# Graph attention on one core: SyncE's row fetches spread over ten turns, VectorE's block loop written out, four widened one-hots in the last block

## The chip, the cores and the metric

The kernel runs as one launch on one core of a Trainium2 chip. The core has five engines that run their own instruction streams and meet only at semaphores: TensorE (PE, with its weight loads shown apart as PEld), VectorE (DVE), ScalarE (ACT), GpSimd (POOL) and SyncE (SP), which computes nothing and issues transfers. The metric is the time of one execution on the device in microseconds (us). Changes of this kernel's time by less than 0.2% are not told from no change.

## The reference, cut to what matters

A graph of 3125 nodes with 128 features and 100000 edges passes through four graph networks. The second (L1) has three attention layers, and the change touches these alone. One layer computes, with edges sorted by destination:

```
xl, xr = h @ Wl + bl, h @ Wr + br                # per node, 4 heads of 32
e      = leaky_relu(xl[dst] + xr[src])           # per edge
logit  = sum over a head's 32 of e * att
alpha  = softmax of logit over the edges of one destination node
out    = segment_sum(alpha * xr[src], dst)
```

Every edge also has the pair of a node with itself, which the kernel adds apart.

## The kernel before, in words

**Tiles.** 125 edges make a tile (one edge per partition), four tiles a quad, so there are 200 quads. The destinations fall into 25 windows of 125 nodes. A step handles one quad for one window; a quad on the border of two windows is handled twice, which gives 224 steps, in 14 blocks of 16 steps. A group is four steps.

**Rows of the sources.** `xr[src]` is gathered row by row (132 numbers: 128 features and 4 more) into `rows`, a ring of 20 quads. GpSimd gathers (`gather_wide`, L615): one indirect DMA fills one tile, and in nine quads out of ten it fetches 128 rows, not 125. The three rows too many, for 36 tiles, are 108 rows of the last tile of the tenth quad, so that quad needs only three gathers. Ten such quads are called a share here (`SHARE`), and SyncE's work on one quad a turn. A layer has 780 gathers.

**SyncE** (`pass_wide`) is the ring's clerk. In each turn q it first frees an old quad: it loads from a table which step uses quad q-18 last, waits until VectorE has weighed it, and raises `kept` (L630). GpSimd waits for `kept` before each quad and may by this be at quad q+2. Then SyncE waits until the rows of quad q have landed and raises `here` (L654), for which VectorE waits. In turn 8 of a share it copies the 108 spare rows into the tenth quad with three DMAs (`hand_over`, L634), and the 17 rows still missing (`ALONE`) it fetches one by one, each with a register loaded from a table (`fetch_alone`, L642): nine in turn 7, behind `here`, and eight in turn 8, behind the hand-over. In turn 9 it waits for all twenty before it raises `here`. After every fourth turn it loads the next list of sources (L625). All this is one stream in order.

**One step on VectorE** has six operations: `z` = destination part (from PSUM `zp`) + rows (L982); `values` = rows times the weights of the step 16 earlier (`weigh`, L995); the leaky relu and the product with `att` (L985); the sum of another earlier step added to `acc` (`add_team`, L1003); the reduction over each head (L988); the logits (L991). Ring slots and windows are run-time numbers, and VectorE loads them into registers for four steps together: 12 numbers ahead of the group's first `z` (`step_places`) and 8 between that and its `weigh` (`step_pairs`).

**One block**: 16 steps, then `softmax(b)`, a chain of small operations that goes back and forth between VectorE, TensorE and ScalarE, up to L1041. There VectorE waits for TensorE (L923, L924), writes `tail` and scales `acc` (L1045 to L1054). In block b the logits of block b and the weighing of block b-1 go side by side. Block 0 only has logits, and behind the last block the 16 steps of weighing stand alone (`close`).

**TensorE** turns one-hots: `spread_rows` (L893) makes `zp` for the next step; `sum_rows` (L903) adds the weighted rows of a step into `sums` with f32 one-hots. **ScalarE** issues the loads of the one-hots from memory (L826, L830) and widens one (bf16 to f32, L835) into one of two buffers `hot32` when the sum two steps earlier is done. A load of a one-hot goes out two steps ahead of its use.

Of the kernel before, what the change touches and what calls it, by code (L numbers as in the profile page):

```python
# [618 lines left out]
def pass_wide(nc, sp, g, table, rows, now, lone, lone_in, staged, rows_in, given, here, kept, step_done, held_up):  # L619

    early = ALONE // 2 + 1
    assert HELD >= GIVING + SHARE - 1 and RING - HELD <= GIVING - 6
# [9 lines left out]
    def hand_over(q):  # L632
        for e in range(EXTRA):
            sp.dma_start(rows[GIVERS * e:GIVERS * (e + 1), q, HALF - 1, :],  # L634
                         rows[P + e:P + e + 1, q - GIVING:q, :, :].rearrange("p a j f -> p (a j) f")).then_inc(given[q // SHARE], 16)

    def fetch_alone(share, q, lo, hi):
# [82 lines left out]
def step_places(nc, eng, g, k, n=AHEAD):  # L720

    _, got = nc.values_load_multi_w_load_instructions(g.place[0:1, bass.ds(3 * k, 3 * n)], engines=(eng.engine,), min_val=0, max_val=QUADS - 1,
                                                      skip_runtime_bounds_check_because="prepare counts them from the step and its window")
    slots = [nc.s_assert_within(v, 0, RING - 1, skip_runtime_bounds_check_because="prepare takes it modulo the ring") for v in got[1::3]]
    wins = [nc.s_assert_within(v, 0, WIN - 1, skip_runtime_bounds_check_because="prepare counts them up from 0, one for each later window") for v in got[2::3]]
    return list(zip(got[0::3], slots, wins))
# [28 lines left out]
def attention(nc, g, table, xl, xr, ft, own_att, own_logit):  # L755
# [4 lines left out]
    with Scope(nc) as sc:  # L760
        rows = sc.sb("rows", [LANES, RING, HALF, ROW])
        now = sc.sb("now", [LANES, STAGES, HALF * HALF], I32)
        lone = sc.sb("lone", [1, QUADS // SHARE * ALONE], I32)
        hot_t = sc.sb("hot_t", [P, AHEAD, HALF * P], BF16)
# [12 lines left out]
        hot32 = sc.sb("hot32", [P, 2, HALF * P])  # L777
        spare = xl[:, :, :].rearrange("p w f -> p (w f)")
# [18 lines left out]
        factor = turn[0:P, 1, 256:256 + D]  # L797
        turned_weights = turn[0:P, 0, 0:HEADS * BT].rearrange("p (h s) -> p s h", h=HEADS)
# [7 lines left out]
        given = [sc.sem(f"given{n}") for n in range(RING // SHARE)]  # L806
        staged = [sc.sem(f"staged{n}") for n in range(STAGES)]
# [7 lines left out]
        @block.sync  # L815
        def _(sp):
            pass_wide(nc, sp, g, table, rows, now, lone, lone_in, staged, rows_in, given, here, kept, weighted, fetching)

        @block.scalar
        def _(act):  # L820
# [11 lines left out]
            def widen(c, m, i, q):  # L832
                act.wait_ge(hot_in[q], landed(m))
                act.wait_ge(closed, after(c, 2))
                act.copy(hot32[:, q % 2, :], hot[:, q, :]).then_inc(made, 1)  # L835
                act.copy(values[:, q % 2, :, D:ACCW], tail[:, bass.ds(HALF * AHEAD * i + HALF * q, HALF), :]).then_inc(tailed, 1)

# [27 lines left out]
            with act.Fori(1, BLOCKS) as b:  # L865
                with act.Fori(0, GROUP) as i:
                    group(b, i)
                weigh(b)
            last = TEAMS - BSTEPS
            with act.Fori(0, GROUP - 1) as i:  # L870
                for q in range(AHEAD):
                    c = last + AHEAD * i + q
                    widen(c, last // AHEAD + i, i, q)
                    load_hot(c + 2, (q + 2) % AHEAD)
            for q in range(AHEAD):
                widen(TEAMS - AHEAD + q, TEAMS // AHEAD - 1, GROUP - 1, q)
                if q < 2:
                    load_hot(TEAMS - AHEAD + q + 2, q + 2)
# [4 lines left out]
        def _(pe):  # L883
# [12 lines left out]
            def sum_rows(c, q):  # L896
                p = q % 2
                pe.wait_ge(made, after(c))
# [3 lines left out]
                for j in range(HALF):  # L902
                    ins = pe.matmul(sums[:, p, 0:ACCW], hot32[:, p, j * P:(j + 1) * P], values[:, p, j, :], start=j == 0, stop=j == HALF - 1)  # L903
# [45 lines left out]
            with pe.Fori(0, GROUP) as i:  # L949
                for q in range(AHEAD):  # L950
                    sum_rows(TEAMS - BSTEPS + AHEAD * i + q, q)

        @block.vector
        def _(dve):
            begin(dve, added, scaled, reduced, summed, weighted, accd)
            link = Link(dve, step)
            link(dve.tensor_copy(factor, own_att))
            for w in range(0, WIN, FIVE):
# [17 lines left out]
            def logits(k, i, q, source):  # L976
                p, s = q % 2, bass.ds(HALF * AHEAD * i + HALF * q, HALF)
                quad, at, _ = source
# [26 lines left out]
            def softmax(b):  # L1005
# [36 lines left out]
                dve.sem_inc(shifted, 1)  # L1042
                first = g.first[:, bass.ds(BT * b, BT)]
# [19 lines left out]
            softmax(0)  # L1063

            def both(b, i):
                first = isinstance(i, int) and i == 0
                for q in range(AHEAD):
                    k = BSTEPS * b + AHEAD * i + q
                    c = k - BSTEPS
                    if q == 0:  # L1070
# [1894 lines left out]
```

## Time and profile before

| what | value |
| --- | --- |
| three runs | 5736.91, 5737.38 (median), 5743.67 us |
| the profiled execution | 5733.8 us, its span 5731.7 us |
| mean granted TensorE clock | 0.799 of full speed |
| the three attention layers, from the first gather to the last sum | 1046.1 to 2177.7, 2231.4 to 3362.6, 3417.5 to 4548.9 us |

The profile shows the profiled execution in microseconds from the start of its span. Each of the layers takes 1131 us, so the part that the change touches is 3394 us of 5732. Busy shares of a whole span average over parts that have nothing to do with each other; an engine's idle time in front of an instruction, and what ended it, say more.

### The profile page before, as it was taken

To read this page: it belongs to the slowest core of one execution; us is meant where nothing else is said; L and a number is where in the kernel's file an instruction comes from. 1 tells how busy PE (TensorE), PEld (TensorE's weight loads), DVE (VectorE), ACT (ScalarE), POOL (GpSimd) and SP (SyncE) were. 2 spreads that over 40 slices of the span, in tenths; PEclk is the share of its full clock that TensorE was granted. 3 is DMA by queue.
4 is the path that set the end of the run, shared out by engine and by line. 5 is a ranking of instruction groups with operands and counts; after the bars stand their busy time and mean duration, and the time that the engine had idled before them with its cause. 6 is when DMAs were issued, how large, how long until landed. Compare 5 with 4: busy or idle time off the path is not lost. (4 is left out here: it accounts for less than half of the span.)

```text
span 5731.7 us, 121544 instructions
## 1 busy us (share of the span) xinstructions
PE 3638.7 (63%) x28023; PEld 3144.2 (55%) x28024; DVE 4068.1 (71%) x8991; ACT 1470.8 (26%) x3625; POOL 2966.9 (52%) x3112
## 2 busy tenths in 40 slices
PE   6887886455555553555565544555555555999985
PEld 5774443355545543545455534555555444999984
DVE  8998523677777777777777777777777657777754
ACT  4775200011111111111111110111111211555553
POOL 0000000566766753767766717767667204777773
PEclk9998997577777776677877766777777777999997
DMA  5883452244434432334444423444434222555552
GB/s 154 220 220 105 129 142 70 67 106 104 104 101 100 105 88 61 99 100 100 104 106 104 103 50 93 104 102 102 102 101 102 56 56 71 144 145 144 144 137 74
DMA packets 528864, 618.70 MB, mean 108 GB/s; under 512 B 123778, under 2 KB 465602, under 8 KB 528740
## 3 DMA queue, kind: packets, MB, share of 16 engines
q0 software_dynamic: 110400, 232.13, 17.7%
q10 hardware_dynamic: 254649, 235.22, 13.8%
q1 hardware_dynamic: 163691, 149.87, 10.0%
q8 instruction: 56, 0.92, 0.1%
q14 instruction: 68, 0.56, 0.0%
HBM read 521.60 MB, written 91.69 MB: 107 GB/s over the span
## 5 line engine op out<-in xcount | busy, mean ns | idle before, releaser
L615 POOL DMA_INDIRECT rows<-row_table,now x2340 | 2269.7, 970 | 1791.3 <-issue 1498.4
L903 PE MATMUL sums<-both,hot 125*125 125x137 f32 x5376 | 1018.9, 345 | 902.1 <-DVE acc L1003 718.6
L903 PEld LDWEIGHTS sums<-both,hot 125*125 125x125 f32 x5376 | 871.5, 235 | 985.3 <-DVE acc L1003 555.4
L600 POOL DMA_INDIRECT rows<-node_table,now x700 | 664.0, 949 | 507.6 <-issue 504.9
L893 PE MATMUL zp<-parts,hot_t 125*125 x8100 | 790.0, 263 | 206.4 <-DVE z L982 110.4
L893 PEld LDWEIGHTS zp<-parts,hot_t 125*125 125x125 bf16 x8100 | 756.0, 173 | 241.2 <-issue 239.6
L835 ACT CAST hot<-hot 125x500 f32<-125x500 bf16 x672 | 408.7, 608 | 1818.0 <-PE sums L903 1630.9
L982 DVE TENSOR_TENSOR z<-zp,rows 125x528 f32<-125x528 f32 x672 | 475.6, 708 | 489.6 <-issue 158.8
L995 DVE TENSOR_TENSOR both<-rows,turn 125x512 f32 (+1 forms) x672 | 457.2, 681 | 89.6 <-issue 46.3
L1278 PE MATMUL mixture<-row_parts,at 125*125 125x384 bf16 x2500 | 446.1, 330 | 45.2 <-DVE at L1335 45.2
L988 DVE TENSOR_REDUCE both<-z 125x16 f32<-125x512 f32 x672 | 457.3, 680 | 4.4
L985 DVE SCALAR_TENSOR_TENSOR z<-z,turn 125x512 f32<-125x512 f32 x672 | 457.7, 681 | 1.7
L1335 DVE TENSOR_TENSOR at<-spread_srcs,nodes 125x1625 bf16<-125x1625 f32 x200 | 356.6, 1784 | 65.0 <-PE mixture L1278 43.9
L1278 PEld LDWEIGHTS mixture<-row_parts,at 125*125 125x125 bf16 x2500 | 330.4, 138 | 104.3 <-issue 25.7
L1614 DVE TENSOR_SCALAR hot<-nodes,both 125x522 bf16<-125x522 f16 x896 | 315.2, 416 | 20.9 <-PE bank L1653 20.7
L1653 PE MATMUL bank<-hot,hot_dst 125*125 125x261 bf16 x1792 | 261.3, 290 | 69.8 <-DVE hot L1614 48.6
L1180 ACT ACTIVATE onehot<-hot,ew 125x125 f32<-125x125 bf16 x896 | 283.1, 387 | 73.1 <-PE zp L1268 42.3
L1372 DVE TENSOR_TENSOR pb<-zp,rows 125x512 f32<-125x512 f32 x224 | 153.9, 687 | 189.8 <-issue 97.7
L1653 PEld LDWEIGHTS bank<-hot,hot_dst 125*125 125x125 bf16 x1792 | 204.8, 139 | 97.0 <-DVE hot L1614 80.0
L1286 PE MATMUL sums<-pb,onehot 125*125 125x129 f32 x1792 | 249.2, 283 | 3.0 <-ACT pb L1186 3.0
L1286 PEld LDWEIGHTS sums<-pb,onehot 125*125 125x125 f32 x1792 | 237.1, 196 | 8.4 <-issue 3.6
L1581 POOL DMA_DIRECT2D spread_slots<-slot_table x56 | 30.2, 539 | 394.8 <-DVE hot_t L1607 339.3
(467 smaller groups left out, 4588.8 us busy)
## 6 DMA issues: line engine op xcount, KB each, us to landing
hot_t<-hots_t ACTq DMA_DIRECT2D x902, 122.1 KB
hot<-hots ACTq DMA_DIRECT2D x896, 122.1 KB
counts<-pairs SPq DMA_DIRECT2D x55, 685.1 KB
rows<-row_table,now POOLq DMA_INDIRECT x2340
spread_slots<-slot_table POOLq DMA_DIRECT2D x56, 488.3 KB, 5.3
hots_t<-hot_t SPq DMA_DIRECT2D x112, 218.8 KB
hots<-hot_dst SPq DMA_DIRECT2D x112, 218.8 KB
pairs<-cells SPq DMA_DIRECT2D x25, 685.1 KB
```

The source lines that it names most:

```text
L600: pool.indirect_dma_start(rows[:, q, j, :], None, table, bass.IndirectOffsetOnAxis(ap=now[:, n, lane + j:lane + j + 1], axis=0)).then_inc( ...
L615: pool.indirect_dma_start(rows[0:lanes, q, j, :], None, table, bass.IndirectOffsetOnAxis(ap=now[0:lanes, n, lane + j:lane + j + 1], axis=0 ...
L835: act.copy(hot32[:, q % 2, :], hot[:, q, :]).then_inc(made, 1)
L893: ins = pe.matmul(zp[:, p, j, 0:ROW], hot_t[:, q, j * P:(j + 1) * P], own[part], start=part == 0 and j % 2 == 0, stop=part == 2, skip_grou ...
L903: ins = pe.matmul(sums[:, p, 0:ACCW], hot32[:, p, j * P:(j + 1) * P], values[:, p, j, :], start=j == 0, stop=j == HALF - 1)
L982: dve.tensor_tensor(z[:, p, :, :], zp[:, p, :, 0:ROW], rows[0:P, bass.ds(at, 1), :, :].rearrange("p a j f -> p (a j) f"), ALU.add).then_in ...
L985: dve.scalar_tensor_tensor(out=z[:, p, :, 0:D], in0=z[:, p, :, 0:D], scalar=0.0, in1=rows_of(factor, HALF), op0=ALU.max, op1=ALU.mult).the ...
L988: dve.tensor_reduce(bent[:, p, :, :], z[:, p, :, 0:D].rearrange("p j (h c) -> p j h c", h=HEADS), AX_X, ALU.add).then_inc(reduced, 1)
L995: dve.tensor_tensor(values[:, q % 2, :, 0:D].rearrange("p j (h c) -> p j h c", h=HEADS), rows[0:P, bass.ds(at, 1), :, 0:D].rearrange("p a ...
L1278: ins = pe.matmul(mixture[:, p, 0:3 * D], hot_n[:, w, :], row_parts[:, w, :, :].rearrange("p k f -> p (k f)"), start=w == 0, stop=w == WIN ...
L1286: ins = pe.matmul(sums[:, q % 2, 0:width], onehot[:, q, j, :], values[:, q % 2, j, :], start=j == 0, stop=j == HALF - 1)
L1653: ins = pe.matmul(bank[0:P, h, 0:CHUNK], hot_dst[:, p, j * P:(j + 1) * P], hot[:, p % AHEAD, j, h * CHUNK:(h + 1) * CHUNK], start=False, s ...
```

## The change

- **SyncE.** The 17 single rows of a share go into a buffer of their own, `alone`, three per turn in turns 0 to 4 and two in turn 5. The hand-over is cut in two: the spare rows of seven quads in turn 7, of the last two in turn 8. In turn 8 SyncE then waits for the 17 rows and copies them into the ring with one DMA. Turn 9 waits for seven transfers, not twenty.
- **VectorE.** The loop over the four groups of a block is written out, 16 steps in one loop body. The registers of a group (8 places, no longer 12, and 8 pairs) are loaded in the middle of a step of the group before, behind `add_team`. The first step's logits of the next block are worked out in the middle of the softmax, between L1041 and the wait for TensorE, with a second copy of `att` in another PSUM bank (`early_factor`).
- **Last block.** Four widened one-hots in place of two (the two more lie in `z`, which is free by then); the first four are widened before the last softmax ends. The later loads of the one-hots are issued by SyncE, four steps ahead. The copy of `tail` and the widening are two functions. The registers are loaded inside the softmax and in the third step of each group.

```diff
-    def hand_over(q):
+    def hand_over(q, lo, hi):
...
-            sp.dma_start(rows[lane:lane + 1, q, HALF - 1, :], table[bass.ds(v, 1), :]).then_inc(given[q // SHARE], 16)
+            sp.dma_start(alone[lane:lane + 1, :], table[bass.ds(v, 1), :]).then_inc(fetched[parity], 16)
...
-                sp.wait_ge(given[share], landed(i, EXTRA + ALONE))
+                sp.wait_ge(given[share], landed(i, 2 * EXTRA + 1))
...
             sp.sem_inc(here, 1)
-            if turn == GIVING - 1:
-                hand_over(q + 1)
-                fetch_alone(RING // SHARE * i + share, q + 1, early, ALONE)
-            if turn == GIVING - 2:
-                fetch_alone(RING // SHARE * i + share, q + 2, 0, early)
+            if each_turn * turn < ALONE:
+                fetch_alone(RING // SHARE * i + share, share, each_turn * turn, min(each_turn * (turn + 1), ALONE))
+            if turn == soon:
+                hand_over(q + 2, 0, soon)
+            if turn == soon + 1:
+                hand_over(q + 1, soon, GIVING)
+                sp.wait_ge(fetched[share], landed(i, ALONE))
+                sp.dma_start(rows[EXTRA * GIVERS:P, q + 1, HALF - 1, :], alone[EXTRA * GIVERS:P, :]).then_inc(given[share], 16)
...
+            with sp.Fori(1, GROUP) as i:
+                for q in range(AHEAD):
+                    c = TEAMS - BSTEPS + AHEAD * i + q
+                    sp.wait_ge(made, after(c, AHEAD))
+                    sp.dma_start(hot[:, q, :], g.hots[bass.ds(c, 1), :, :].rearrange("a p n -> (a p) n")).then_inc(hot_in[q], 16)
...
+            def widen_late(c, m, q):
+                act.wait_ge(hot_in[q], landed(m))
+                act.wait_ge(closed, after(c, AHEAD))
+                act.copy(wide_hot[q], hot[:, q, :]).then_inc(made, 1)
...
                 dve.sem_inc(shifted, 1)
+                if meanwhile is not None:
+                    meanwhile()
...
+                softmax(b - 1, meanwhile=first_logits)
+                weigh(BSTEPS * b - BSTEPS, 0, 0, ahead["pairs", 0][0][0])
+                for i in range(GROUP):
+                    for q in range(1 if i == 0 else 0, AHEAD):
...
+                                if i < GROUP - 1 and q == AHEAD - 2:
+                                    load_places(i + 1)
+                                if i < GROUP - 1 and q == AHEAD - 1:
+                                    load_pairs(i + 1)
```

## Rows read from the trace of the kernel before

**Rows 1.** The page's busy times: engine, us, share of the span, instructions.

```profile
PE 3638.7 (63%) x28023; PEld 3144.2 (55%) x28024; DVE 4068.1 (71%) x8991; ACT 1470.8 (26%) x3625; POOL 2966.9 (52%) x3112
```

**Rows 2.** The gathers by layer: ns min/median/max, first to last start; idle ended by L630.

```profile
L615 POOL DMA_INDIRECT rows<-row_table,now x780: 938/944/1511, 1046.1 to 2117.5; - x195
...
  SPq L630: 96.6, 65
...
L615 POOL DMA_INDIRECT rows<-row_table,now x780: 938/944/1357, 2231.4 to 3302.2; - x195
...
  SPq L630: 99.2, 72
...
L615 POOL DMA_INDIRECT rows<-row_table,now x780: 938/944/1347, 3417.5 to 4488.4; - x195
...
  SPq L630: 97.0, 63
```

**Rows 3.** POOL in order of time at one share's end: start, us, [idle before].

```profile
1573.28 0.94 POOL L615 DMA_INDIRECT rows<-row_table,now  x1 [0.30 <-issue]
...
1588.06 0.94 POOL L615 DMA_INDIRECT rows<-row_table,now  x1 [4.23 <-SPq L630]
```

**Rows 4.** SyncE's DMA issues in the same stretch.

```profile
1573.61 3.63 SPq L642 DMA_DIRECT2D rows<-row_table  x9
1578.40 2.36 SPq L634 DMA_DIRECT2D rows<-rows  x3
1583.18 3.16 SPq L642 DMA_DIRECT2D rows<-row_table  x8
```

**Rows 5.** VectorE in order of time: starts of z around two groups' first steps.

```profile
1561.45 0.71 DVE L982 TENSOR_TENSOR z<-zp,rows 125x528 f32<-125x528 f32 x1 [1.71 <-PE zp L893]
...
1565.27 0.71 DVE L982 TENSOR_TENSOR z<-zp,rows 125x528 f32<-125x528 f32 x1 [0.41 <-DVE both L991]
...
1571.86 0.71 DVE L982 TENSOR_TENSOR z<-zp,rows 125x528 f32<-125x528 f32 x1 [0.28 <-DVE both L991]
...
1576.65 0.71 DVE L982 TENSOR_TENSOR z<-zp,rows 125x528 f32<-125x528 f32 x1 [1.77 <-issue]
```

**Rows 6.** VectorE from one softmax to the next, with the join to the next block.

```profile
1593.40 0.30 DVE L1003 TENSOR_TENSOR acc<-acc,sums 125x137 f32 x1 [0.89 <-PE sums L903]
...
1603.32 0.22 DVE L1041 TENSOR_SCALAR delta<-delta,joined 1x4 f32<-1x4 f32 x1
1606.84 0.43 DVE L1045 COPY xl<-turn 125x256 f32<-125x256 f32 x1 [3.31 <-PE sums L924]
...
1613.71 0.71 DVE L982 TENSOR_TENSOR z<-zp,rows 125x528 f32<-125x528 f32 x1 [0.29 <-DVE both L991]
...
1669.11 0.30 DVE L1003 TENSOR_TENSOR acc<-acc,sums 125x137 f32 x1 [0.88 <-PE sums L903]
```

**Rows 7.** The end of the first layer's gathers, and the last step's z.

```profile
2117.52 1.19 POOL L615 DMA_INDIRECT rows<-row_table,now  x1 [0.30 <-issue]
...
2128.02 0.71 DVE L982 TENSOR_TENSOR z<-zp,rows 125x528 f32<-125x528 f32 x1 [4.91 <-SPq L654]
```

**Rows 8.** The last 16 sums of the first layer, all engines in order of time.

```profile
2148.04 1.28 DVE L995 TENSOR_TENSOR both<-rows,turn 125x512 f32<-125x512 f32 x2 [0.95 <-DVE acc L1054]
...
2148.97 4.85 PE L903 MATMUL sums<-both,hot 125*125 125x137 f32 x24 [3.37 <-ACT both L836]
...
2155.52 1.20 PE L903 MATMUL sums<-both,hot 125*125 125x137 f32 x8 [0.26 <-ACT both L836]
...
2156.57 0.61 ACT L835 CAST hot<-hot 125x500 f32<-125x500 bf16 x1 [1.24 <-DMA hot<-hots]
...
2177.41 0.30 DVE L1003 TENSOR_TENSOR acc<-acc,sums 125x137 f32 x1 [1.28 <-PE sums L903]
```

**Rows 9.** Code loads from 1250 to 2100 us; a large transfer's us to landing.

```profile
q14 instruction: 1, 0.01, 0.0%
...
spread_slots<-slot_table POOLq DMA_DIRECT2D x56, 488.3 KB, 5.3
```

More of the change, by code:

```diff
@@ L720, in step_places @@
 def step_places(nc, eng, g, k, n=AHEAD):
-    _, got = nc.values_load_multi_w_load_instructions(g.place[0:1, bass.ds(3 * k, 3 * n)], engines=(eng.engine,), min_val=0, max_val=QUADS - 1,
+    _, got = nc.values_load_multi_w_load_instructions(g.place[0:1, bass.ds(2 * k, 2 * n)], engines=(eng.engine,), min_val=0, max_val=QUADS - 1,
                                                       skip_runtime_bounds_check_because="prepare counts them from the step and its window")
-    slots = [nc.s_assert_within(v, 0, RING - 1, skip_runtime_bounds_check_because="prepare takes it modulo the ring") for v in got[1::3]]
-    wins = [nc.s_assert_within(v, 0, WIN - 1, skip_runtime_bounds_check_because="prepare counts them up from 0, one for each later window") for v in got[2::3]]
-    return list(zip(got[0::3], slots, wins))
+    slots = [nc.s_assert_within(v, 0, RING - 1, skip_runtime_bounds_check_because="prepare takes it modulo the ring") for v in got[1::2]]
+    return list(zip(got[0::2], slots))
 def step_pairs(nc, eng, g, k):
@@ L797, in attention @@
         factor = turn[0:P, 1, 256:256 + D]
+        early_factor = sums[:, 1, 256:256 + D]
         turned_weights = turn[0:P, 0, 0:HEADS * BT].rearrange("p (h s) -> p s h", h=HEADS)
@@ L868, in _ @@
                 weigh(b)
+            with act.Fori(0, GROUP) as i:
+                group(BLOCKS - 1, i)
             last = TEAMS - BSTEPS
+            act.wait_ge(closed, after(last - 1))
+            for q in range(2):
+                widen_late(last + q, last // AHEAD, q)
+                load_hot(last + q + 2, q + 2)
+            act.wait_ge(summed, after(TEAMS - 1))
+            for q in range(2, AHEAD):
+                widen_late(last + q, last // AHEAD, q)
+            weigh(BLOCKS - 1)
+            copy_tail(last, 0, 0)
             with act.Fori(0, GROUP - 1) as i:
@@ L872, in _ @@
                     c = last + AHEAD * i + q
[L873 to L878, printed above, removed]
+                    copy_tail(c + 1, i, q + 1)
+                    widen_late(c + AHEAD, last // AHEAD + 1 + i, q)
+            for q in range(1, AHEAD):
+                copy_tail(TEAMS - AHEAD + q, GROUP - 1, q)
             for q in range(2):
@@ L1062, in _ @@
                         pass
[L1063 to L1070, printed above, removed]
-                        sources = step_places(nc, dve, g, k)
-                    for stage, _ in enumerate(logits(k, i, q, sources[q])):
-                        if stage == 0:
-                            if q == 0:
-                                pairs = step_pairs(nc, dve, g, c)
-                            weigh(c, i, q, pairs[q][0])
-                        elif stage == 1 and (q > 1 or not first):
-                            add_team(c - 2, (q - 2) % AHEAD, pairs[q][1])
@@ L1086, in _ @@
                     add_team(BSTEPS * b - 2 + q, q + 2, ws[q])
-                softmax(b)
+            with dve.Fori(1, BLOCKS) as b:
+                both(b)
             last = TEAMS - BSTEPS
-            def close(i):
-                pairs = step_pairs(nc, dve, g, last + AHEAD * i)
+            pairs = []
+            softmax(BLOCKS - 1, meanwhile=lambda: pairs.append(step_pairs(nc, dve, g, last)))
+            for i in range(GROUP):
                 for q in range(AHEAD):
                     c = last + AHEAD * i + q
-                    weigh(c, i, q, pairs[q][0])
-                    if q > 1 or not isinstance(i, int):
-                        add_team(c - 2, (q - 2) % AHEAD, pairs[q][1])
-            close(0)
-            with dve.Fori(1, GROUP) as i:
-                close(i)
+                    weigh(c, i, q, pairs[i][q][0])
+                    if q > 1 or i > 0:
+                        add_team(c - 2, (q - 2) % AHEAD, pairs[i][q][1])
+                    if q == 2 and i < GROUP - 1:
+                        pairs.append(step_pairs(nc, dve, g, last + AHEAD * (i + 1)))
             ws = windows_of(nc, dve, g, TEAMS - 2, 2)
```

67 lines of the change are left out of this document (46 added, 21 removed).

## The prediction

> **What bounds the kernel now.** The page's busy times come first, and they mislead: VectorE at 71% and GpSimd at 52% look as if VectorE set the pace [rows 1]. Both are averages over parts in which GpSimd has nothing to do. So next I read the gathers' line within each layer [rows 2]. In the first layer 780 gathers run from 1046.1 us to the end of the last at 2118.7, 1072.6 us; the other layers take 1072.0 and 1072.1. In order of time one gather takes 0.94 us and the next follows 0.30 later whatever happens [rows 3]: 780 such pairs are already 970 us. GpSimd thus issues nearly without a break, and what it waits for costs time. That is in the second lines of rows 2: idle time that ended at L630, SyncE's release of a quad, 96.6 us in 65 waits. Each includes the usual gap of 0.30, so what is really lost is 96.6 - 65 x 0.30 = 77.1 us; in the other layers 99.2 - 21.6 = 77.6 and 97.0 - 18.9 = 78.1. Without this a layer's gathers take 995 us, or 995 / 14 = 71.1 us per block of 16 steps.
>
> Where the loss sits is seen by laying GpSimd and SyncE side by side [rows 3, 4]. GpSimd stops before the second quad of a share, until 1588.06, for 4.23 us. SyncE in the meantime issues nine single rows (3.63 us), the hand-over (2.36), then loads eight registers (1580.76 to 1583.18, 2.42) and issues eight more rows (until 1586.34). Only then does it come to turn 9, whose release GpSimd waits for. The stop is thus SyncE's own work, in order, in front of a release.
>
> VectorE is not far behind. From softmax to softmax it takes 1669.11 - 1593.40 = 75.7 us [rows 6]. It has to be shortened as well, or it becomes the bound: 75.7 is more than 71.1.
>
> **SyncE, costed.** Before, turn 7 issues nine rows (3.63 us) and loads nine registers (at 2.42 / 8 = 0.30 each, 2.7 us): 6.3 us ahead of turn 8's release. After, only the hand-over's three DMAs stand there, 2.36 us [rows 4]. Turn 8 before: 2.36 + 2.42 + 3.16 = 7.9 us ahead of turn 9's release. After: 2.36, a wait for 17 rows whose last was issued two turns earlier, and one DMA of 0.4 us (a single row's) to 0.8 (a hand-over's): 3.2 at most. Turn 8's release comes 3.9 us earlier and turn 9's at least 4.7, more than the stop of 4.23. What is moved has to be paid in turns 0 to 5: three registers (0.9) and three DMAs (1.2), 2.1 us behind `here`, against four gathers of 1.25, 5.0 us; and GpSimd is up to two quads ahead, so it doesn't feel them. Queued behind the new wait for the 17 rows are one copy and turn 9's release, so if the rows were late the old stop would be back; they have more than a turn, some 5 us. I take the whole loss as gone: 77.1 + 77.6 + 78.1 = 232.8 us. Bounds: half of it (116) if the spread work stops GpSimd elsewhere, and no more than all of it, because a gather and its gap don't get shorter.
>
> At a layer's end the same work lies between the last gather (ends 2118.71) and the last `z` (2128.02), 9.3 us, with VectorE waiting for L654 for 4.91 of them [rows 7]. Of turn 8's work the registers and eight rows go (5.6) and one copy comes (0.4 to 0.8): 5 us less, per layer, between 3 and 7 since the last rows have to land anyway.
>
> **VectorE, costed.** It only has to fall below 71.1 us per block. In the middle of a group a step takes (1571.86 - 1565.27) / 2 = 3.30 us. Into a group's first step it is 1576.65 - 1571.86 = 4.79, out of it 1565.27 - 1561.45 = 3.82 [rows 5]: 1.49 + 0.52 = 2.0 us for registers, three times per block within the loop. After, the loads stand behind `add_team`, where VectorE still has the leaky relu and the sum in hand; I take 0.2 us per load as not hidden, six loads, 1.2, and 2.0 x 3 as gone. Bounds: 0 and the full 6.0 remaining. The join: L1041 ends at 1603.54, and the second `z` of the block starts at 1613.71, 10.2 us later, of which 3.31 are a wait for TensorE [rows 6]. After, places, first `z`, pairs and the three other operations fall into that wait: about 1.0 + 3.0 us, so L1045 starts some 0.6 us late, near 1607.5; its group takes the 1.5 that it takes now, `weigh` 0.6, and `z` comes at 1609.8: 3.9 us gained. The block: 75.7 - 6.0 + 1.2 - 3.9 = 67.0 us, 4 below the gathers' 71.1. As long as this holds, VectorE waits for rows, and what it gains beyond is worth nothing. If it is held up in a softmax, the gathers go on: SyncE can free quads weighed in the block before, about four quads or 20 us, against a softmax of some 14.
>
> Code is loaded too: in 850 us of the first layer's loops there is a single code transfer in the queues shown [rows 9], so the loops now run without it. The Trainium skill (Runtime: NRT & Kernel Launch, section Instruction fetch mechanics) speaks against this change: a taken branch to a page of code that is no longer held waits for a transfer, and a loop body of 16 written-out steps may no longer fit. No row here shows such a wait; what one would cost in this kernel is worked out from rows as the third rival.
>
> **The last block.** Before, the first weighing is 0.95 us late for registers, which now load inside the softmax: 0.95 gained. From the first sum (2148.97) to the end (2177.71) are 28.7 us [rows 8]. ScalarE waits for the one-hot's DMA (1.24 us), since the load goes out only two steps ahead. Four ahead, TensorE and the add set the pace: a sum of 1.20 and 0.26 of gap, 1.46. The first three sums took 4.85; with thirteen at 1.46 and 0.5 for the last add it comes to 24.3: 4.4 gained, between 0 (the DMA still late) and 8 (1.2 per sum).
>
> **The sum.** 232.8 + 3 x (5 + 0.95 + 4.4) = 263.9 us. The profiled execution took 5733.8, which gives 5469.9; it lies 3.6 below the median of the three runs, 5737.4, so the forecast for a median is **5473 us**, 4.6% faster. Loads ahead of the first gather and all that follows the third layer stay as they are.
>
> **The rivals.**
> 1. *VectorE becomes the bound.* If the registers are hidden not at all, a block costs 75.7 - 3.9 = 71.8, and with the join worth only 2.7 it is 73. Each microsecond over 71.1 costs 13 x 3 = 39 us: 28 to 75 us more, 5500 to 5548. For it: a margin of only 4 us in 67. Against it: if 12 numbers hold a step up by 1.49, 8 take about 1.0, and the work in front of a step's reduction is about half of its 3.30.
> 2. *The stop at the share's end stays in part*, because SyncE is late from another side (the hand-over of seven quads now precedes turn 8's release), so that half of it is left: 116 us less gain, 5590. For it: the queue is in order as before. Against: both releases come earlier by the sums above.
> 3. *Code transfers.* One transfer for each loop-back, priced between nothing and the 5.3 us that 488 KB take to land [rows 9]: 67.0 + 5.3 = 72.3, 1.2 over the gathers, 47 us more, 5520. Under 4 us it stays within the margin and changes nothing. For it: a longer loop body. Against it: only a price at the far end of the bounds counts.
> 4. *Slower.* The same mechanism, several times per block: the written-out body is loaded again in pieces in each turn of the loop, and VectorE waits for each piece. The gain of 264 us is used up when a block takes 71.1 + 264 / 39 = 77.9 us, so from 10.9 us of such waits per block on (two at 5.4, or three at 3.6); at 80 us per block the kernel takes 5473 + 8.9 x 39 = 5820. For it: 16 steps in place of four in the inner loop. Against it: straight-line code runs in this kernel too, and the waits of rows 6, in a stretch without a loop, end in an engine's work and not in code.
>
> **How the numbers follow.** The forecast, gathers without stops, gets 0.68 and has its own range of 5455 to 5495 (close and tail at their bounds, 3 x 4 to 8 us). Rival 1 gets 0.12 and rival 3 0.06 (5495 to 5550), rival 2 0.10, slower 0.03, and 0.01 for a change that comes out within 0.2%. Low end: all of the stops gone, with 7 and 8 us at the layers' ends, 5737.4 - 233 - 3 x 16 = 5456; I go to 5450. The high end takes in most of rivals 1 and 3: 5540. A change of less than 0.2% (11 us) can't be told from none. Faster 0.96, same 0.01, slower 0.03.
>
> **What would show it.** Right: in each layer the gathers last 990 to 1000 us from first to last, waits on SyncE's release nearly only the usual 0.30; VectorE waits at `z` for L654 in most blocks, some 4 us per block, since it is the faster one; `z` follows the last gather in 4 to 5 us; the last 16 sums take 22 to 26 us. Wrong, if VectorE's idle time ends in "issue" several us long once per block (code), if blocks take over 71 us with no wait for `here` (rival 1), or if POOL still stands for over 1 us before a share's first or second quad (rival 2). It would be wrong as a whole if a gather with its gap took longer than 1.25 us under the denser traffic.

## The result: 5495.06 us, 0.9577 of before, and the profile after

The changed kernel takes 5495.06 us (median of four, 5489.47 to 5499.54); before took 5737.15 (four, 5733.05 to 5743.67). The ratio is 0.9577, 95% interval 0.956 to 0.9593. The forecast was 5473, range 5450 to 5540: the sign and the range held, and the point lies 22 us too low. The time alone tells little of the cause: 5495 is the upper end of the forecast's own range and the lower end of that of rivals 1 and 3.

The profiled execution of after took 5489.47 us, its span is 5487.7 against 5731.7, so 244.0 us less. First the page's busy times and code queue of after (packets, MB, share of 16 engines):

```profile
PE 3504.3 (64%) x28023; PEld 2996.9 (55%) x28024; DVE 4057.2 (74%) x8992; ACT 1471.7 (27%) x3625; POOL 2967.0 (54%) x3112
...
q14 instruction: 195, 1.60, 0.1%
```

VectorE's, ScalarE's and GpSimd's busy times are nearly those of [rows 1]: on these engines the change took away waiting, not work. (TensorE's fell by 134 us; its mean granted clock is 0.822 in this execution and was 0.799.) How much of it, and where, the gathers' line shows for each layer, as in [rows 2]: ns min/median/max, first and last start, and the idle time that ended in SyncE's release, now L631.

```profile
L615 POOL DMA_INDIRECT rows<-row_table,now x780: 938/944/1597, 1039.1 to 2058.4; - x195
...
  SPq L631: 42.3, 63
...
L615 POOL DMA_INDIRECT rows<-row_table,now x780: 938/944/1354, 2159.3 to 3152.6; - x195
...
  SPq L631: 14.0, 46
...
L615 POOL DMA_INDIRECT rows<-row_table,now x780: 938/944/1380, 3252.9 to 4256.4; - x195
...
  SPq L631: 23.6, 43
```

To the end of the last gather these are 1020.5, 994.5 and 1004.7 us, where before had some 1072 each. Less the usual 0.30 per wait, GpSimd loses 23.4, 0.2 and 10.7 us to releases, where it lost 77 to 78. The three layers run the same code on the same edges, so they should agree, and they did before. The second layer's gathers are the forecast to the microsecond; the first's and third's are not. Cut at three points, in us (gathers from first start to last end; last gather's end to last `z`; last `z` to the end of the last sum; all of it):

| layer | gathers | to last `z` | to last sum | layer |
| --- | --- | --- | --- | --- |
| before: 1, 2, 3 | 1072.6, 1072.0, 1072.1 | 9.3, 8.5, 9.3 | 49.7, 50.7, 50.0 | 1131.6, 1131.2, 1131.4 |
| after: 1, 2, 3 | 1020.5, 994.5, 1004.7 | 4.7, 3.6, 4.1 | 40.2, 39.9, 40.6 | 1065.4, 1038.0, 1049.4 |

The differences of the last column, 66.2 + 93.2 + 82.0 = 241.4 us, are all but 2.6 of what the span lost.

What differs between the layers is seen in VectorE's waits, grouped by line and by what ended them (us in total, times, longest), in after's first, second and third layer:

```profile
DVE brk L1044 <- issue: 35.3, 13, 3.4
DVE xl L1048 <- issue: 25.0, 12, 2.5
...
DVE z L1017 <- SPq L655: 20.0, 21, 3.8
...
DVE z L1017 <- SPq L655: 52.7, 30, 3.8
...
DVE brk L1044 <- issue: 2.8, 13, 0.2
...
DVE z L1017 <- SPq L655: 45.1, 33, 3.2
...
DVE brk L1044 <- issue: 34.4, 13, 3.3
```

L1044 is the first operation of the softmax, hence of the loop's body, and 13 is the number of its turns; the first turn is entered without a jump back and has only 0.2 us of the wait, so the rest falls on twelve jumps. In the second layer VectorE passes from one turn to the next without a stop, and waits for rows (L655) at `z`: it is the faster engine, as forecast. In the third it idles some 2.8 us after each jump back ((34.4 - 0.2) / 12 = 2.85 on average), in the first 2.9 and then 2.1 at L1048, the next operation, 5.0 together, and "issue" says that no engine and no transfer shown held it up. In order of time, VectorE at two turns' starts in the first layer, one in the third and two in the second:

```profile
1486.73 0.39 DVE L1044 CAST brk<-brk 64x126 f32 x1 [2.74 <-issue]
1489.01 0.41 DVE L1048 TENSOR_TENSOR_SCAN xl<-brk,turn 64x125 f32<-64x125 f32 x1 [1.89 <-issue]
...
1562.80 0.32 DVE L1044 CAST brk<-brk 64x126 f32 x1 [2.80 <-issue]
...
3767.14 0.22 DVE L1044 CAST brk<-brk 64x126 f32 x1 [2.74 <-issue]
...
2668.50 0.22 DVE L1044 CAST brk<-brk 64x126 f32 x1 [0.21 <-issue]
...
2681.76 0.42 DVE L1082 COPY xl<-turn 125x256 f32<-125x256 f32 x1
...
2748.53 0.41 DVE L1082 COPY xl<-turn 125x256 f32<-125x256 f32 x1
```

The code queue moves with it. Its transfers in the first, second and third layer of after:

```profile
q14 instruction: 70, 0.57, 0.2%
...
q14 instruction: 11, 0.09, 0.0%
...
q14 instruction: 72, 0.59, 0.2%
```

These are about five transfers of 8 KB per turn where VectorE stops, and hardly any where it doesn't. The trace's own record of the branch that ends the loop (L1136) agrees: VectorE's next instruction starts 2.9 and 2.8 us behind it (medians of the first and third layer), and 0.2 in the second. So this was the theory to be tested: VectorE's loop, 328 instructions where before's outer loop had 209, is fetched anew at each jump back in two of the three layers, depending on where in the program its copy of the code begins (each layer has a copy of its own). The rivals were that the lower gain comes from SyncE (stops that stay), from VectorE's registers, or from the last block.

SyncE itself does what was planned. Its transfers in the second layer at a share's end, and GpSimd in the same stretch:

```profile
2599.89 2.50 SPq L635 DMA_DIRECT2D rows<-rows  x3
2602.61 0.37 SPq L626 DMA_DIRECT2D now<-tile_src  x1
2605.36 2.08 SPq L635 DMA_DIRECT2D rows<-rows  x3
2607.56 0.65 SPq L663 DMA_DIRECT2D rows<-alone  x1
2616.22 7.92 SPq L643 DMA_DIRECT2D alone<-row_table  x6
```

```profile
2603.93 1.33 POOL L615 DMA_INDIRECT rows<-row_table,now  x1 [0.30 <-SPq L631]
2620.15 0.94 POOL L615 DMA_INDIRECT rows<-row_table,now  x1 [0.30 <-SPq L631]
```

The nine and eight single rows of [rows 4] no longer stand between two hand-overs; one copy of 0.65 us does. GpSimd passes the stop of 4.23 us [rows 3] with the usual 0.30.

### The profile page after: what moved, and what is told of

It reads as the page before. It is cut to its first block and busy times, and to the rows that moved or that the text cites. A ratio compares the mean times of both kernels' runs of the same rounds, so it can differ in the third digit from the quotient of the medians.

```text
span 5487.7 us, 121476 instructions
## 1 busy us (share of the span) xinstructions
PE 3504.3 (64%) x28023; PEld 2996.9 (55%) x28024; DVE 4057.2 (74%) x8992; ACT 1471.7 (27%) x3625; POOL 2967.0 (54%) x3112
## 5 line engine op out<-in xcount | busy, mean ns | idle before, releaser
L937 PE MATMUL sums<-both,hot 125*125 125x137 f32 x5184 | 895.0, 323 | 678.5 <-DVE acc L1038 583.5
L937 PEld LDWEIGHTS sums<-both,hot 125*125 125x125 f32 x5184 | 764.0, 216 | 752.1 <-issue 392.9
L926 PE MATMUL zp<-parts,hot_t 125*125 x8100 | 737.3, 250 | 241.8 <-DVE z L1017 109.4
L926 PEld LDWEIGHTS zp<-parts,hot_t 125*125 125x125 bf16 x8100 | 684.7, 159 | 295.2 <-issue 292.5
L848 ACT CAST hot<-hot 125x500 f32<-125x500 bf16 x624 | 379.5, 608 | 1418.0 <-PE sums L937 836.2
L1030 DVE TENSOR_TENSOR both<-rows,turn 125x512 f32<-125x512 f32 x672 | 456.1, 679 | 28.1 <-PE sums L937 18.2
L1020 DVE SCALAR_TENSOR_TENSOR z<-z,turn 125x512 f32<-125x512 f32 x633 | 431.5, 682 | 1.7
L1383 DVE TENSOR_TENSOR at<-spread_srcs,nodes 125x1625 bf16<-125x1625 f32 x200 | 356.6, 1784 | 64.1 <-PE mixture L1326 40.6
L1701 PEld LDWEIGHTS bank<-hot,hot_dst 125*125 125x125 bf16 x1792 | 204.8, 139 | 96.5 <-DVE hot L1662 75.7
L862 ACT ACTIVATE xl<-xl 64x500 f32<-64x500 f32 x42 | 26.0, 619 | 803.9 <-DVEq L1077 803.9
```

The source lines that it names most:

```text
L926: ins = pe.matmul(zp[:, p, j, 0:ROW], hot_t[:, q, j * P:(j + 1) * P], own[part], start=part == 0 and j % 2 == 0, stop=part == 2, skip_grou ...
L937: ins = pe.matmul(sums[:, p, 0:ACCW], hots[:, j * P:(j + 1) * P], values[:, p, j, :], start=j == 0, stop=j == HALF - 1)
L1020: dve.scalar_tensor_tensor(out=z[:, p, :, 0:D], in0=z[:, p, :, 0:D], scalar=0.0, in1=rows_of(factor, HALF), op0=ALU.max, op1=ALU.mult).the ...
L1030: dve.tensor_tensor(values[:, q % 2, :, 0:D].rearrange("p j (h c) -> p j h c", h=HEADS), rows[0:P, bass.ds(at, 1), :, 0:D].rearrange("p a ...
L1383: dve.tensor_tensor(hot_n[:, lo:hi, :], src, each(nodes[:, lo:hi], P), ALU.is_equal).then_inc(noded, 1)
L1701: ins = pe.matmul(bank[0:P, h, 0:CHUNK], hot_dst[:, p, j * P:(j + 1) * P], hot[:, p % AHEAD, j, h * CHUNK:(h + 1) * CHUNK], start=False, s ...
```

## Experiments

Medians of four or five runs; ratios are to the kernel before, run beside them, whose medians were 5736.87 to 5739.26. They ran in three sets: the parts undone and `pad` first; `unroll_old_last`, `lanes` and `unroll_lanes_noearly` last.

**Each part undone.** `old_sync` has before's `pass_wide`, with the single rows in turns 7 and 8:

```diff
-            if each_turn * turn < ALONE:
-                fetch_alone(..., share, each_turn * turn, min(each_turn * (turn + 1), ALONE))
...
+            if turn == GIVING - 1:
+                hand_over(q + 1)
+                fetch_alone(..., q + 1, early, ALONE)
+            if turn == GIVING - 2:
+                fetch_alone(..., q + 2, 0, early)
```

> The changed kernel with SyncE's turns as they were before (17 single rows in turns 7 and 8); VectorE's blocks and the last block stay as changed. My theory: GpSimd's gathers set the pace, and SyncE's burst alone made them stop at each share's end. So the stops come back whole although VectorE is faster: the gathers of every layer take about 1072 us again, waits on SyncE's release some 97 us per layer, and with 9.3 us from the last gather to the last z the kernel takes 5690 to 5710. The rival, that VectorE's lateness in freeing quads made half of the stops, gives about 5600.

Measured: 5714.21 us, 0.9957 [0.9941, 0.9972]. VectorE's and ScalarE's parts without SyncE's are worth 25 us. Releases and the rows' landing in its second layer:

```profile
DVE z L1011 <- SPq L654: 140.4, 57, 7.5
...
POOL rows L615 <- SPq L630: 93.3, 63, 4.4
```

The stops are back (93.3 - 63 x 0.30 = 74 us), and a faster VectorE only waits longer for rows. That layer takes 1116.9 us against 1038.0: 74 of stops and 5 at the layer's end make up the 78.9. Its first and third layers load code too (70 and 71 transfers) and take 1135.5 and 1126.4 us, and the time came out a little above the 5690 to 5710 that were expected.

`old_vector` has the loop over groups and the registers at a group's start, as before:

```diff
-            with dve.Fori(1, BLOCKS) as b:
-                both(b)
+            with dve.Fori(1, BLOCKS) as b:
+                both(b, 0)
+                with dve.Fori(1, GROUP) as i:
+                    both(b, i)
+                softmax(b)
```

> The changed kernel with VectorE's blocks as before: a loop over groups of four steps, registers loaded at a group's start, no logits inside the softmax; SyncE and the last block stay as changed. My theory: VectorE then needs 75 to 76 us per block, over the gathers' 71, and becomes the bound: 13 x 4.5 us per layer more than a layer bound by gathers, so 5620 to 5660. Its loop is short (209 instructions), so no code is loaded again and all three layers are alike. The rival, that SyncE's part alone brings the gain and VectorE's part is worth nothing, gives 5490 to 5500.

Measured: 5604.21 us, 0.9766 [0.9752, 0.9781], below the expected stretch. VectorE's waits for `z` in the second layer:

```profile
DVE z L1017 <- issue: 77.7, 61, 1.7
...
DVE z L1017 <- SPq L655: 5.6, 7, 1.4
```

The wait for rows is nearly gone (52.7 us in after) and 77.7 us of idle time in "issue", where the registers are loaded, stand in its place: now VectorE is the bound. Its gathers take 1037.5, 1039.1 and 1037.4 us, 74.1 per block and not 75.7; that it loads 8 places per group and not 12 fits this, and was not tried alone. All layers alike, and no more than 12 code transfers in any: the short loop is not fetched again. GpSimd's stops are back too (some 40 us per layer), this time most of them behind VectorE's softmax.

`old_last` has before's last block, two widened one-hots with ScalarE's loads two steps ahead:

```diff
-            with sp.Fori(1, GROUP) as i:
-                for q in range(AHEAD):
-                    c = TEAMS - BSTEPS + AHEAD * i + q
-                    sp.wait_ge(made, after(c, AHEAD))
-                    sp.dma_start(hot[:, q, :], ...)
...
-                    sum_rows(TEAMS - BSTEPS + AHEAD * i + q, q, late=True)
+                    sum_rows(TEAMS - BSTEPS + AHEAD * i + q, q)
```

> The changed kernel with the last block as before: two widened one-hots, their loads issued by ScalarE two steps ahead, registers loaded at each group's start. In the trace of the changed kernel the time from the last z to the last sum is 40 us where it was 49.7. If that is the last block's part and not something that SyncE or VectorE's blocks brought, it is 49 to 50 us again in each layer and the kernel takes 27 to 29 us more, 5520 to 5526. By the forecast's own term it would be 16 us more, 5511.

Measured: 5551.46 us, 0.9676 [0.9661, 0.9691], far above. From the last `z` to the last sum it takes 48.0 to 49.6 us, 8.5 more than after on average, which was the aim. But the change also moved the code that follows: the second layer now idles 35.1 us in "issue" at the softmax's first operation and 19.9 at the scan, with 71 code transfers, and takes 1070.7 us where after's took 1038.0; in the third VectorE's stops are gone, but GpSimd still loses 12.6 us, with 50 code transfers, and there it is SyncE's loop that waits at its jump back (see `unroll_old_last` below). The run says little on the last block and much on the code's place.

**Only the code moved.** `pad` puts instructions that only count up a semaphore nobody waits for ahead of VectorE's part of a layer: 8, 0 and 48 in the three layers. Each runs once; they shift the loop's code and do nothing else.

```diff
+FILLERS = (8, 0, 48)
...
+            for _ in range(FILLERS[layer]):
+                dve.sem_inc(filler, 1)
```

> The changed kernel with 8 filler instructions on VectorE (each raises a semaphore that nobody waits for) ahead of the first layer's work and 48 ahead of the third's, none in the second. Nothing else moves but the place of VectorE's block loop in its code. My theory: what the first and third layer take more than the second (27 and 11 us) is code loaded again in every turn of the loop, because there the loop of 328 instructions lies over four pieces of 8 KB and not over three as in the second layer; shifted, all three lie over three. The q14 code transfers in the three layers' loops fall from about 60 to nearly none, VectorE's idle time ahead of L1044's line vanishes, each layer takes 1037 to 1040 us and the kernel 5452 to 5462. The rival, that the first and third layer are slower for a reason of their own (their data, their neighbours in memory traffic), leaves 5490 to 5500.

Measured: 5490.51 us, 0.9567 [0.9554, 0.958], far above the 5452 to 5462 expected, and in the range of the rival, by which the place of the code doesn't matter. The layers say otherwise: they had changed places. The first and third layers' turn starts, and what GpSimd lost in the third:

```profile
DVE brk L1050 <- issue: 3.0, 13, 0.3
...
DVE brk L1050 <- issue: 64.3, 13, 5.8
POOL rows L615 <- SPq L631: 46.5, 66, 5.0
```

Eight fillers cure the first layer: 1040.8 us where it took 1065.4. Forty-eight make the third worse: 5.3 us of stop per jump back, 1071.1 us where it took 1049.4. `pad2` takes 70 there:

```diff
-FILLERS = (8, 0, 48)
+FILLERS = (8, 0, 70)
```

> As the kernel with fillers, but 70 in front of the third layer in place of 48 (8 in front of the first, none in front of the second). With 48 the first layer lost its code loads (layer 1065 to 1041 us) and the third got a second stop per turn of the loop (1049 to 1071): so its loop began just ahead of a piece's border, and 22 instructions on it begins behind it and lies over three pieces. My theory: 5455 to 5465, with 1038 to 1042 us in each layer and under 4 us in all of idle time in front of the block's first operation. The rival, that the third layer is slow for a reason of its own, leaves it at 1049 or more, 5468 or more.

Measured: 5460.54 us, 0.9514 [0.9501, 0.9527], as expected. Layers of 1040.5, 1042.2 and 1045.4 us, 10 to 13 code transfers in each (the third is above the 1038 to 1042 expected; GpSimd has a single stop of 4.2 us early in it), and in the third:

```profile
DVE brk L1050 <- issue: 3.3, 13, 0.3
```

Seventy-eight instructions more than after, and 34.5 us less in the medians.

**No jump back.** In `unroll` all 13 turns are written out one after the other:

```diff
-            with dve.Fori(1, BLOCKS) as b:
-                both(b)
+            for b in range(1, BLOCKS):
+                both(b)
```

> The changed kernel with VectorE's loop over the 13 blocks written out as well: 13803 instructions on VectorE, no jump back in the blocks. The same code stands on no loop, so nothing is read twice, but all of it is read once. If it is the jump back that waits for code, code in sequence comes in time and every layer takes 1037 to 1042 us, wherever its code lies: 5452 to 5464. The rival, that VectorE waits for code whenever it is new, gives stops of 2 to 3 us in each 8 KB (some 33 of them in a layer) and 5495 or more.

Measured: 5457.1 us, 0.9508 [0.9495, 0.9521], as expected. Gathers of 994.1, 995.4 and 993.9 us, 0.2 us lost to releases in each layer. In the first:

```profile
DVE z L1017 <- SPq L655: 66.4, 44, 3.8
...
POOL rows L615 <- SPq L631: 12.2, 40, 0.3
```

Code is still fetched (35 or 36 transfers per layer), but in sequence, and VectorE stops for none of it. So the transfer by itself stopped nothing here; the stops go with the jump back.

`unroll_noearly` is `unroll` without the logits in the softmax; the first step of a block follows the join, as before:

```diff
-                softmax(b - 1, meanwhile=first_logits)
-                weigh(BSTEPS * b - BSTEPS, 0, 0, ahead["pairs", 0][0][0])
+                softmax(b - 1)
+                load_places(0)
+                load_pairs(0)
```

> The kernel with all blocks written out, but without the first step's logits inside the softmax: they stand behind it again, with their registers loaded there. My theory: this gives VectorE 4 to 5 us more per block, 66.8 becomes 71 to 72, just at the gathers' 71, so that the kernel loses little: 0 to 40 us against the one with all blocks written out. The rival, that VectorE's path counts in full since it is the bound in every block, gives 13 x 3 x 4.3 = 168 us more.

Measured: 5460.44 us, 0.9516 [0.9503, 0.9529], 3 us more than `unroll`. VectorE again waits 3.3 us for TensorE in each block (second line below), but most of that only changes places. In `unroll`'s second layer a later `z` waits for TensorE's `zp` instead (last line), here nearly never (0.3 us in all). Less its waits for rows a block takes 66.1 us here and 64.7 in `unroll`: 1.4 more, not the 4 to 5 of the expectation, and the gathers hardly notice. `unroll_noearly` and then `unroll`, second layers:

```profile
DVE z L1017 <- SPq L655: 65.2, 44, 3.8
DVE xl L1082 <- PE sums L958: 46.3, 14, 3.3
...
POOL rows L615 <- SPq L631: 14.0, 46, 0.3
...
DVE z L1017 <- PE zp L926: 42.6, 25, 3.2
```

**The last block alone.** `unroll_old_last` undoes the last block where VectorE has no block loop that could move:

```diff
-            with dve.Fori(1, BLOCKS) as b:
+            for b in range(1, BLOCKS):
...
-                    sum_rows(TEAMS - BSTEPS + AHEAD * i + q, q, late=True)
+                    sum_rows(TEAMS - BSTEPS + AHEAD * i + q, q)
```

> The kernel with all blocks written out, and the last block as before (two widened one-hots, loads issued by ScalarE, registers at each group's start). With the last block undone in the changed kernel itself the time went up by 56 us, but in that trace the second layer then loaded code again in every turn of its loop, since the shorter code ahead of it moved the loop. My theory: the last block alone is 8 to 10 us per layer (last z to last sum 48 to 50 us, not 40), the rest of the 56 was the moved code; without a loop it is 24 to 30 us, 5481 to 5487. The rival, that the last block is really worth 56, gives 5513.

Measured: 5487.91 us, 0.9572 [0.9559, 0.9585], 30.8 above `unroll` and 1 above what was expected. From the last `z` to the last sum it takes 47.2, 49.4 and 48.5 us, against 40.4, 41.0 and 40.5: 23.2 over three layers, 7.7 each. The rest is mostly GpSimd's: 11.2 us of stops in the third layer, where 76 code transfers appear again, although VectorE's code runs in sequence. The trace tells whose code it is. At the jump back of SyncE's own loop over 20 quads (L674), SyncE's next instruction starts 2.5 to 4.9 us behind the branch at all eight jumps of this layer, 25.9 us in sum, and 0.2 us behind it in the other two layers and in every layer of `unroll`. One such jump ends at 3846.53 us, SyncE goes on at 3851.40 and raises the release (L631) at 3852.14; GpSimd:

```profile
3852.95 0.94 POOL L615 DMA_INDIRECT rows<-row_table,now  x1 [3.58 <-SPq L631]
```

All seven stops of this layer over 0.9 us lie behind such a jump. `old_last` has the same in its third layer. Undoing the last block also takes the one-hots' loads out of SyncE's code, so SyncE's loop had moved, too.

**The gathers themselves.** With GpSimd unhindered, only its own line is left. In order of time, a gather at the second layer's end in after, and one in the middle of the first in `unroll_lanes`:

```profile
3149.62 1.21 POOL L615 DMA_INDIRECT rows<-row_table,now  x1 [0.30 <-issue]
```

```profile
1485.65 0.94 POOL L615 DMA_INDIRECT rows<-row_table,now  x1 [0.30 <-issue]
```

The slow ones are those of a share's tenth quad, which fetch 125 rows; all others fetch 128 (and some 13 of those 720 per layer are slow as well). There are three per share, 60 per layer. `lanes` and `unroll_lanes` let them fetch 128 as well, three of which nobody reads, on after and on `unroll`:

```diff
-            lanes = LANES if giving else P
+            lanes = LANES
```

> The kernel with all blocks written out, and in the tenth quad of a share the three gathers fetch 128 rows like all others and not 125 (the three more are not used). In the traces a gather of 125 rows takes 1.20 us, one of 128 takes 0.94. If the gathers are the bound, 60 of them per layer save 0.26 us each: 15.6 us per layer, 47 us in all, so 5405 to 5420. If VectorE is the bound in the block, or the length of a gather doesn't matter, nothing is gained.

Measured: 5407.88 us, 0.9427 [0.9414, 0.944], as expected: 49 us below `unroll`, 87 below after. Gathers of 978.1, 978.9 and 979.1 us, 16 less per layer; 60 x (1.20 - 0.94) is 15.6. More rows in less time.

> The changed kernel with 128 rows in every gather, nothing written out and no fillers. My theory: only a layer that is bound by its gathers gains. The second layer (no code loaded in its loop) falls by 15 us to 1022 to 1026; the first, where VectorE waits twice per block for code, gains 0 to 6, the third 0 to 12: 5495 becomes 5465 to 5482. The rival, that each layer gains its 15.6 us, gives 5448.

Measured: 5459.77 us, 0.9518 [0.9505, 0.9531], 35 below after, and a little below the 5465 to 5482 expected. The gathers now need only 69.9 us per block: gathers of 1014.4, 979.1 and 990.5 us, with 35.3, 0.9 and 10.8 lost to releases. The second layer, which fetches no code, gains 15.4; the first, where VectorE sets the pace, 6.1. The third gains 14.2 and loses to releases what it lost before, which the expectation (0 to 12) had too low.

`unroll_lanes_noearly` is `unroll_noearly` with the same edit, to see how near VectorE is to the bound:

```diff
-                softmax(b - 1, meanwhile=first_logits)
+                softmax(b - 1)
...
-            lanes = LANES if giving else P
+            lanes = LANES
```

> The kernel with all blocks written out and 128 rows in every gather, without the first step's logits inside the softmax. With gathers of 995 us per layer those logits were worth 3 us in all. With 979 the gathers need 69.9 us per block, and VectorE without the early logits about 71: my theory is that now VectorE sets the pace, and the logits are worth 20 to 60 us, 5428 to 5468. The rival, that VectorE still has time left, gives 5408 to 5414.

Measured: 5416.37 us, 0.9443 [0.9431, 0.9456], 8.5 above `unroll_lanes` and less than expected. VectorE waits for rows still 48 to 51 us per layer. GpSimd has three stops over 1 us in the three layers and loses 3.2, 0.2 and 2.4 us.

## Why the prediction was right, and where 22 us went

**SyncE, right.** 232.8 us were forecast for the stops. Where no code is fetched they go whole: 0.2 us is left in after's second layer and in all of `unroll`'s, with gathers of 994 to 995 us, the 995 that the prediction worked out. Rival 2 falls: `old_sync` brings the stops at a share's end back; the stops that after still has in two layers lie behind VectorE's softmax (below). The layer's end, forecast at -5, came to -4.6, -4.9 and -5.2.

**VectorE, right in sum, with the join mis-sized.** From one L1082 to the next it takes 2748.53 - 2681.76 = 66.8 us in the second layer, in the block with the least waiting for rows (0.3 us); 67.0 was forecast. On average a block of that layer takes 70.6 us, of which 52.7 / 13 = 4.1 are waits for rows. Inside the sum two terms were off and made up for each other. Before's third `z` behind a softmax, then after's softmax's last step, its second `z` and its third:

```profile
1616.82 0.71 DVE L982 TENSOR_TENSOR z<-zp,rows 125x528 f32<-125x528 f32 x1 [0.28 <-DVE both L991]
...
2677.89 0.22 DVE L1076 TENSOR_SCALAR delta<-delta,joined 1x4 f32<-1x4 f32 x1
...
2683.96 0.70 DVE L1017 TENSOR_TENSOR z<-zp,rows 125x528 f32<-125x528 f32 x1
...
2689.33 0.71 DVE L1017 TENSOR_TENSOR z<-zp,rows 125x528 f32<-125x528 f32 x1 [2.56 <-PE zp L926]
```

From the end of this step the second `z` comes after 5.85 us, where before took 10.2 [rows 6]: 4.3 gained, as forecast (3.9). But then the third `z` waits for TensorE, and up to there only 1616.82 - 1603.54 = 13.3 less 2689.33 - 2678.11 = 11.2, 2.1 us, are gained. By subtraction the other 6.8 us of 75.7 - 66.8 come from the rest of the block, where the registers were to give 4.8. That the sum came out to 0.2 us is thus partly luck.

Two limits show that the block had to be shortened and that more is worth little: at 74.1 us (`old_vector`) VectorE is the bound and 109 us of the gain are lost, and 1.4 us more per block (`unroll_noearly`) cost 3 us in all. Rival 1 falls: the registers at the groups' starts are hidden.

**Code, the step that failed.** The sum had nothing for code. Rival 3, a code transfer per loop-back, had 0.06, with a price up to 5.3 us and nothing to pay below 4. It came true in two of three layers, with the sign that the prediction had named for it ("issue" several us long once per block). A jump back costs 2.8 us in the third, and 5.0 in the first, where VectorE stops a second time. In the first a block less its waits for rows takes 71.4 us, over the 71.1, and the ring stops GpSimd for 23 us. But in the third it takes 68.3, within the margin (66.7 in the second), and the gathers still take 10 us longer, in five stops of 1.4 to 4.1 us. Each ends where VectorE weighs for the first time behind a softmax:

```profile
3710.04 0.69 DVE L1030 TENSOR_TENSOR both<-rows,turn 125x512 f32<-125x512 f32 x1 [0.23 <-DVE acc L1091]
3711.57 0.94 POOL L615 DMA_INDIRECT rows<-row_table,now  x1 [4.14 <-SPq L631]
```

So "under 4 us it stays within the margin" failed because it compared averages. What counts is how long VectorE frees no quad. From the last weighing ahead of a softmax to the first behind it are 17.9 to 18.7 us in the second layer, without a stop, 20.8 to 21.9 in the third and 22.5 to 23.3 in the first, with eleven. The prediction had set "a softmax of some 14" against the 20 us that the ring lasts; the 20 fits the runs, the 14 was too small, and only some 2 us were to spare, less than one jump back costs.

`pad`, `pad2` and `unroll` show that it is the place of the code and the jump: from after to `pad2`, which only adds fillers, 34.5 us are gained. That the loop was fetched anew because its pieces reach over one more border is the reading that fits, and the pieces' borders themselves were not seen.

The Trainium skill (Runtime: NRT & Kernel Launch, section Instruction fetch mechanics) says that a taken branch to a page not in the two-page window waits for a fetch, and gives this as one reason why kernels prefer full unrolling. The runs agree: 2.8 us per jump in after's third layer, no such stop of VectorE in `unroll`. What they add is that one loop of 328 instructions pays in one copy and not in the other.

**The last block, right in kind and mis-sized.** The term of 4.4 us for the 16 sums was too small. In after's second layer TensorE's first and last sums, and the last add:

```profile
3176.96 3.56 PE L937 MATMUL sums<-both,hot 125*125 125x137 f32 x16 [2.31 <-DVE both L1030]
...
3182.73 2.46 PE L937 MATMUL sums<-both,hot 125*125 125x137 f32 x16
3185.07 2.48 PE L937 MATMUL sums<-both,z 125*125 125x137 f32 x16
...
3194.51 2.37 PE L937 MATMUL sums<-both,z 125*125 125x137 f32 x16
...
3197.02 0.30 DVE L1038 TENSOR_TENSOR acc<-acc,sums 125x137 f32 x1 [0.89 <-PE sums L937]
```

From first sum to end 3197.32 - 3176.96 = 20.4 us: 8.3 less than the 28.7 of [rows 8], the far end of the bound given (8), and under the 22 to 26 that the prediction had named as its sign. Two sums take 2.4, back to back. The gap of 0.26 that the forecast added to each came from a row that waits for L836, ScalarE's copy of `tail`; the change moves that copy out of the way, so the row was no guide. In all, the last `z` to the last sum fell by 9.5, 10.8 and 9.4 us, where 0.95 + 4.4 was forecast; `unroll_old_last` puts 7.7 of it on the last block itself; where the other 2 us or so come from was not told apart.

**How the two misses add up.** The last block gave (9.9 - 5.35) x 3 = 13.7 us more than forecast, which would have made 5459.3; `pad2` and `unroll`, which pay no code stops, measured 5460.54 and 5457.1. The code stops take 34.5 back: 5459.3 + 34.5 = 5493.8, and 5495.06 was measured. It closes better than the runs allow: the profiled executions of after and `pad2`, the fastest of four and the slowest of five, are only 25.6 us apart, so the code's share is known to some 10 us.

## What to carry to other kernels

Once a loop body grows, look for idle time that ends in "issue" at its first operation, turn by turn, and for transfers on the code queue in the same stretch; if they are there, write the loop out, or move its code, before anything else is tuned. Look at every engine that has a loop: an edit can move SyncE's code as well as VectorE's. When a ring lies between two engines, compare the longest stretch in which the slower side frees nothing with what the ring holds; an average per block hides it. When copies of the same code take different times on the same work, the copies' place is the first suspect. When an engine that issues without a break has become the bound, its own instructions are the next thing to price, each form apart: here, fetching three useless rows took another 49 us off `unroll`, which with it is 5.7% faster than before.

## What the hardware showed unexpectedly

- An indirect gather of 125 rows held GpSimd 1.20 us, one of 128 rows 0.94. With the 60 such gathers of a layer changed to 128, a layer's gathers went from 994 or 995 to 978 or 979 us. Why was not tried.
- The same VectorE loop of 328 instructions cost 0.2, 2.8, 5.0 or 5.3 us at its jump back, by its place in the code; 22 instructions ahead of it (48 or 70 fillers) were worth 26 us in one layer (1071.1 against 1045.4).
- Code in sequence, 35 transfers of 8 KB per layer, held VectorE up nowhere that the profile shows.
- SyncE's loop paid as well where an edit had moved its code: 2.5 to 4.9 us at each of eight jumps back in `unroll_old_last`'s third layer.
